# Score-table blanks on one DMA queue, and edge groups scored one place further up

## The chip, the cores and the metric

The kernel runs on one core of a Trainium2 chip. The metric is the device time of the whole program in microseconds, the median of several runs.

## The reference, cut to what matters

The program is two layers of a graph model on 625 nodes of width 256 with 20,000 edges. The first half of layer 0 holds two branches that share the engines. The edge branch gives each of the 20,000 edges four attention scores:

```python
e = xl[src] + xr[dst]                      # xl = xn @ W_l, xr = xn @ W_r
e = jnp.where(e >= 0, e, 0.2 * e)
score = jnp.einsum('ehd,hd->eh', e, att)   # then a softmax over the edges of each dst
```

The mix branch is dense: layer norm, `Wx`, a small linear attention over all nodes (`Wq`, `Wk`, `Wv`, `Wo`), a second layer norm, and a GELU MLP of width 1024. After these come the dense softmax of the edge scores, an expert layer, and the whole of layer 1; none of that is touched by the change.

## The kernel before, in words

The edges are cut into 32 groups of 5 x 125 edges. Groups 0 to 11 are "early": their scoring is written in between the pieces of the mix branch. Groups 12 to 31 are "late" and run in a loop of their own. All order is written by hand: each engine has one program in order and waits on semaphores.

An early group `g` takes these steps. `hot_rows(g)` on ACT turns the loaded destination indices into one-hot rows (10 activations, it needs `node_neg`). `early_rows(g, ...)` on PE multiplies them with `xr`, in three pieces of 20, 10 and 20 matmuls (line 481), into PSUM banks 5 to 7. POOL gathers the five columns of `xl[src]` from the DRAM table `xl_tab` (line 1778). DVE adds both (`add_rows`, line 909), applies the leaky ReLU and the weights and sums (`score_rows`, lines 887, 892, 895), and copies the indices of group `g + 2` (line 872). `score_early(g)` is both. POOL's `turn(g)` then scatters the scores of group `g - 2` to the DRAM tables `pair_scores` (line 1788) alternately with the gathers of group `g`, ten instructions in all:

```python
pool.wait_ge(sem("indices"), g + 1)
pool.wait_ge(sem("scored"), g - 1)
```

Both score tables (6.1 MB each) must first be filled with a large negative number. These are the blanks: ten DMAs of 1093.8 and 127.0 KB for each table, read from the SBUF tile `cnt`. POOL waits for both tables before its first scatter. Before the change SP sends the first table and ACT the second, after ACT has seen the `xl_tab` stores land.

`count_group(g, s)` on PE (line 459, 25 matmuls) counts edges per node pair from one-hots that DVE makes in `onehots(g, s)` (lines 944 and 945, ten instructions). PE does `count_group` 0 to 7 between the last early groups; a late group `g` on PE waits for the one-hots of group `g - 4`.

## Time and profile before

| what | value |
|---|---|
| median of 3 runs | 1266.75 us (1263.19 to 1271.56) |
| the profiled execution | 1262.88 us |
| its span, first to last instruction | 1261.1 us |
| PE busy | 961.6 us (76%) |
| DVE busy | 781.7 us (62%) |
| ACT busy | 468.5 us (37%) |
| POOL busy | 454.4 us (36%) |
| granted TensorE clock, mean | 0.876 of full speed |

The shares are averages over stages that differ. The change touches the stretch from 0 to about 250 us, so the windows and the chain of waits of that stretch tell more than the table. Times in the rows below are microseconds from the start of the span.

### The profile page before, as it was taken

To read this page: it belongs to the slowest core of one execution; us is meant where nothing else is said; L and a number is where in the kernel's file an instruction comes from. 1 tells how busy PE (TensorE), PEld (TensorE's weight loads), DVE (VectorE), ACT (ScalarE), POOL (GpSimd) and SP (SyncE) were. 2 spreads that over 40 slices of the span, in tenths; PEclk is the share of its full clock that TensorE was granted. 3 is DMA by queue.
4 is the path that set the end of the run, shared out by engine and by line. 5 is a ranking of instruction groups with operands and counts; after the bars stand their busy time and mean duration, and the time that the engine had idled before them with its cause. 6 is when DMAs were issued, how large, how long until landed. Compare 5 with 4: busy or idle time off the path is not lost.

```text
span 1261.1 us, 19695 instructions
## 1 busy us (share of the span) xinstructions
PE 961.6 (76%) x6816; PEld 836.3 (66%) x6816; DVE 781.7 (62%) x1821; ACT 468.5 (37%) x786; POOL 454.4 (36%) x371
## 2 busy tenths in 40 slices
PE   4387999699898988746328999908891982999992
PEld 2356887598797977546328899805781772788881
DVE  6368479777869889798663444234988757233312
ACT  2045756567766965255111111101540240111110
POOL 1448788877777778400002222140000000111103
PEclk9688999899999999957659999958895995899996
DMA  8932222222222222294036889840000003576662
GB/s 288 290 120 64 62 69 73 58 65 62 63 60 65 63 58 43 50 245 109 1 106 223 295 303 304 299 143 0 1 1 0 1 1 111 197 269 238 253 219 70
DMA packets 57996, 155.86 MB, mean 124 GB/s; under 512 B 23341, under 2 KB 33506, under 8 KB 49674
## 3 DMA queue, kind: packets, MB, share of 16 engines
q1 hardware_dynamic: 25500, 116.31, 28.0%
q0 software_dynamic: 25056, 24.10, 8.5%
q10 hardware_dynamic: 7378, 14.67, 3.5%
q8 instruction: 34, 0.56, 0.2%
q14 instruction: 28, 0.23, 0.1%
HBM read 133.82 MB, written 20.89 MB: 123 GB/s over the span
## 4 chain that ended last, share of the span: by engine, by line
PE 48%; DVE 22%; DMA 11%; issue 8%; POOL 6%; ACTq 2%; ACT 1%; another core or an unknown queue 0%; DVEq 0%; POOLq 0%; SPq 0%
PE bank L697 13%; PE bank L481 8%; PE bank L708 6%; DMA arena<-row_tab,ids 5%; DMA pair_scores<-sc_ring,idx_ring 4%; PE bank L645 4%; PE bank L459 4%; PE bank L443 3%; PE bank L433 3%; POOL arena L1778 2%; PE bank L634 2%; POOL pair_scores L1788 2%; POOL arena L1843 2%; ACTq L1586 2%; PE bank L762 1%
## 5 line engine op out<-in xcount | busy, mean ns | idle before, releaser
L1833 POOL DMA_INDIRECT arena<-row_tab,ids x42 | 58.7, 1398 | 573.9 <-DVE ids L1355 503.9
L1788 POOL DMA_INDIRECT pair_scores<-sc_ring,idx_ring x160 | 204.4, 1278 | 68.2 <-issue 48.8
L697 PE MATMUL bank<-arena 128*128 128x128 f32 (+1 forms) x1616 | 198.1, 280 | 0.0
L697 PEld LDWEIGHTS bank<-arena 128*128 128x128 f32 (+1 forms) x1616 | 186.3, 189 | 7.7 <-issue 3.6
L1778 POOL DMA_INDIRECT arena<-xl_tab,idx_ring x120 | 157.9, 1316 | 90.5 <-issue 33.2
L1367 DVE TENSOR_TENSOR arena<-bank,arena 128x512 f32<-128x512 f32 (+2 forms) x76 | 37.2, 509 | 151.9 <-ACT arena L1671 151.9
L708 PE MATMUL bank<-arena 128*128 128x256 f32 (+1 forms) x404 | 99.0, 388 | 0.0
L1558 ACT ACTIVATE late_ohT<-arena 125x875 fp32r<-125x875 f32 x100 | 90.7, 928 | 0.0
L1671 ACT ACTIVATE arena<-bank 128x512 f32<-128x512 f32 (+2 forms) x76 | 32.4, 450 | 148.1 <-PE bank L697 148.1
L481 PE MATMUL bank<-late_hi,late_ohT 125*125 125x256 f32 x500 | 85.9, 303 | 0.4 <-issue 0.3
L708 PEld LDWEIGHTS bank<-arena 128*128 128x128 f32 (+1 forms) x404 | 72.0, 190 | 16.6 <-issue 9.2
L459 PE MATMUL bank<-tde 125*128 125x314 bf16 x400 | 65.6, 318 | 19.9 <-DVE tde L945 19.0
L481 PE MATMUL bank<-late_lo,late_ohT 125*125 125x256 f32 x500 | 77.4, 285 | 0.1
L481 PEld LDWEIGHTS bank<-late_hi,late_ohT 125*125 125x125 f32 x500 | 70.4, 194 | 3.3 <-issue 0.5
L459 PE MATMUL bank<-tab 125*128 125x314 bf16 x400 | 61.3, 303 | 14.5 <-DVE tab L945 14.3
L1654 ACT ACTIVATE arena<-bank 128x256 f32<-128x256 f32 x42 | 16.1, 384 | 149.9 <-PE bank L684 135.4
L1626 ACT ACTIVATE arena<-arena,rneg 125x625 f32<-125x625 f32 (+4 forms) x60 | 44.8, 747 | 72.0 <-DVE rneg L1198 69.2
L481 PEld LDWEIGHTS bank<-late_lo,late_ohT 125*125 125x125 f32 x500 | 67.9, 190 | 0.5 <-issue 0.4
L645 PE MATMUL bank<-xlr,arena 125*125 125x96 f32 x400 | 57.9, 300 | 10.6 <-ACT arena L1634 10.5
L459 PEld LDWEIGHTS bank<-tde 125*128 125x128 bf16 x400 | 38.7, 103 | 38.0 <-DVE tde L945 21.0
L645 PEld LDWEIGHTS bank<-xlr,arena 125*125 125x125 f32 x400 | 55.1, 218 | 11.5 <-ACT arena L1634 11.2
L1345 DVE TENSOR_TENSOR arena<-iota_s,slot_rel 125x1280 f16<-125x1280 f16 x42 | 62.5, 1488 | 0.3
(307 smaller groups left out, 1923.6 us busy)
## 6 DMA issues: line engine op xcount, KB each, us to landing
arena<-in_exp SPq DMA_DIRECT2D x25, 1024.0 KB, 5.5
arena<-in_exp SPq DMA_DIRECT2D x17, 1364.0 KB
arena<-in_exp0o SPq DMA_DIRECT2D x25, 512.0 KB, 5.4
arena<-pair_scores SPq DMA_DIRECT2D x10, 1093.8 KB
arena<-in_exp1o SPq DMA_DIRECT2D x17, 640.0 KB
pair_scores<-cnt SPq DMA_DIRECT2D x5, 1093.8 KB
pair_scores<-cnt ACTq DMA_DIRECT2D x5, 1093.8 KB
slot_y<-arena ACTq DMA_DIRECT2D x42, 128.0 KB, 5.0
```

The lines of the kernel that those rows point to most:

```text
L433: mm = pe.matmul(bank[0:P, 0:width], f[:, k, t * P:(t + 1) * P], rhs(k), start=(k == 0), stop=(k == ks - 1))
L459: mm = pe.matmul(banks[m][:, 0:CW], oh_dst[s][:, j, m * P:m * P + 128], oh_src[s][:, j, :], start=start and j == 0, stop=True, skip_group_ ...
L481: mm = pe.matmul(banks[T + r][0:P, i * D:(i + 1) * D], hot[late, s][:, t, at * P:(at + 1) * P], part[:, t, :], start=(n == 0 and t == 0), ...
L645: mm = pe.matmul(banks[b][0:P, h * 128:h * 128 + VW], probT[:, i % 3, t * P:(t + 1) * P], v_rows(t, h), start=(t == 0), stop=(t == tiles_o ...
L697: mm = pe.matmul(banks[1 + 2 * q + buf][0:rows, i * SLOTS:(i + 1) * SLOTS], w_in(s, q, k, m, rows), xsT[:, s, k, :], start=(k == 0), stop= ...
L708: mm = pe.matmul(banks[5 + s][:, 0:D], hid[0:rows, s, m, :], w_out(s, m), start=(m == 0), stop=(m == len(flat) - 1))
L1345: v.tensor_tensor(sel[:, s, :, :], iota_s[:, :].unsqueeze(1).to_broadcast([P, 2 * T, SLOTS]), slot_rel[:, :].unsqueeze(2).to_broadcast([P, ...
L1558: ins = a.activation(hot[late, s][:, t - 1, :], apart[late, s][:, t - 1, :], ACT.Relu, scale=-1.0, bias=1.0)
L1626: a.activation(prob[:, i % 3, 0:w], masked[:, i % 3, 0:w], ACT.Exp, bias=rneg[:, i:i + 1], accum_out=rden[:, i:i + 1]).then_inc(sem(name + ...
L1778: p.indirect_dma_start(out=gat[:, b % 2, 0, j * D:(j + 1) * D], out_offset=None, in_=xl_tab, in_offset=bass.IndirectOffsetOnAxis(ap=idx_ri ...
L1788: p.indirect_dma_start(out=pair_scores[which], in_=sc_ring[:, b % 2, j, :], in_offset=None, out_offset=bass.IndirectOffsetOnAxis(ap=idx_ri ...
L1833: p.indirect_dma_start(out=xs[:, s, :], out_offset=None, in_=tab, in_offset=bass.IndirectOffsetOnAxis(ap=ids[:, s, :], axis=0))\
```

## The change

The blanks of the second table move from ACT's queue to SP's, behind the `xl_tab` stores and two loads of index rows, with three weight loads behind them (`vec0b`, `w0b`, `w2`). The twelve small loads of `mixw` and `mixk` move from SP's queue to the head of ACT's program, ahead of its first activation. The `xl_tab` store is cut into five per-tile stores. `node_neg` is made at the start, so that ACT can do `hot_rows(0)` and `hot_rows(1)` early. In the mix branch each early group is scored one place further up: group 0 before `mixhT` is copied out, group 1 before the `qv` copies, and so on. At the end of the early groups PE loses one place: `count_group(5)` now stands ahead of `early_rows(11)`.

```diff
@@ PE
-            pe.wait_ge(sem("w0_in"), 16)
             pe.wait_ge(sem("mixh"), 1)
             to_fm("mixhT", ta)
+            early_rows(1, 0, 1, 2)
+            pe.wait_ge(sem("w0_in"), 16)
...
-            early_rows(7, 0, 1, 2)
+            early_rows(8, 0, 1, 2)
             read_out(pe, "m2")
             count_group(0, 0)
             count_group(1, 1)
-            early_rows(8, 0, 1, 2)
+            early_rows(9, 0, 1, 2)
             count_group(2, 0)
             count_group(3, 1)
-            early_rows(9, 0, 1, 2)
+            early_rows(10, 0, 1, 2)
             count_group(4, 0)
-            early_rows(10, 0, 1, 2)
             count_group(5, 1)
             early_rows(11, 0, 1, 2)
             count_group(6, 0)
@@ DVE
+            dve.wait_ge(sem("iotas"), 5)
+            v.tensor_scalar(node_neg[:, :], node_f[:, :], -1.0, None, ALU.mult).then_inc(sem("node_neg"), 1)
             dve.wait_ge(sem("x_in"), 16 * len(PARTS))
...
             affine(ta, 0, "ln1_g", "ln1_b", sem("mixh"))
-            own.note(v.tensor_tensor(tb[:, :, :], xn[:, :, :], V(0, "bo"), ALU.add))
+            score_early(0)
             from_fm("mixhT", fb_)
...
-            score_early(0)
+            own.note(v.tensor_tensor(tb[:, :, :], xn[:, :, :], V(0, "bo"), ALU.add))
+            score_early(1)
...
-            score_early(9)
+            score_early(10)
             onehots(5, 1)
             take_counts(0, early, True)
-            score_early(10)
             onehots(6, 0)
+            score_early(11)
             onehots(7, 1)
-            score_early(11)
             onehots(8, 0)
@@ ACT
+            act.wait_ge(sem("mixw0"), 1)
+            for q in range(4):
+                rows = slice(32 * q, 32 * q + 32)
+                act.dma_start(mixw[rows, q, :], mixw_in[:, 0:KR + DH]).then_inc(sem("mixw_in"), 16)
+                for k in range(K2):
+                    at = (4 * k + q) * KR
+                    act.dma_start(mixk[rows, k, at:at + KR], mixw_in[:, KR + DH:]).then_inc(sem("mixw_in"), 16)
             from_fm("xnT0", fa)
             act.wait_ge(sem("node_neg"), 1)
             hot_rows(0, 0, 0)
-            act.wait_ge(sem("tables"), 16 * len(PARTS))
-            for m in range(T):
-                for rows in PARTS:
-                    act.dma_start(cells[1][m][rows], cnt[rows, :, :].rearrange("p m n -> p (m n)")[:, 0:H * NC])\
-                        .then_inc(sem("blank1"), 16)
...
+            hot_rows(1, 1, 0)
             from_fm("mixhT", fb_)
@@ SP
-            blank_first()
-            read_out(sp, "lr")
-            for rows in PARTS:
-                sp.dma_start(xl_tab.rearrange("(t p) d -> p t d", p=P)[rows], xlr[rows, :, 0:D])\
-                    .then_inc(sem("tables"), 16)
+            blank(0, range(T))
             sp.dma_start(vec[:, 0:V_FIRST], vec0_in[0:V_FIRST].partition_broadcast(128)).then_inc(sem("vec0_in"), 16)
+            for t in range(T):
+                read_out(sp, "lr", t)
+                for rows in PARTS:
+                    sp.dma_start(xl_tab[t * P:(t + 1) * P, :][rows], xlr[rows, t, 0:D]).then_inc(sem("tables"), 16)
...
             for g in range(2, 4):
                 edge_rows(g, g % 2, 0)
+            blank(1, range(T))
```

Three places of the program show it. The first is ACT's start, as a difference: line 1583 and 1586 are the small loads, `fa` receives the first transposed activations, which the product for `xl` and `xr` needs.

```order
 L1531 UNCONDITIONAL_BRANCH
+L1583 DMA mixw<-in_mixw 32x36
+L1586 DMA mixk<-in_mixw 32x4 x2
+L1583 DMA mixw<-in_mixw 32x36
+L1586 DMA mixk<-in_mixw 32x4 x2
+L1583 DMA mixw<-in_mixw 32x36
+L1586 DMA mixk<-in_mixw 32x4 x2
+L1583 DMA mixw<-in_mixw 32x36
+L1586 DMA mixk<-in_mixw 32x4 x2
 L1539 ACT_TABLE_LOAD
 L1539 ACTIVATE fa<-bank 128x375
```

Twelve DMA issues now stand ahead of the table load and the copy to `fa`.

The second is DVE behind the first layer norm of the mix branch. Before (`fb` receives `mixhT`, `fc` receives `Wx`'s output):

```order
L851 TENSOR_TENSOR tab<-tab,vec 125x1280 [waits dve_own]
L1050 TENSOR_TENSOR tab<-xn,vec 125x1280
L868 COPY fb<-bank 128x375 [waits full1]
L868 COPY fb<-bank 128x250 [waits full2]
L1055 TENSOR_SCALAR fc<-bank,fbias 128x375 [waits full0,fb_in]
L1055 TENSOR_SCALAR fc<-bank,fbias 128x250 [waits full1]
L909 TENSOR_TENSOR arena<-arena,bank 125x512 [waits z_made,gathered0]
```

Now:

```order
L851 TENSOR_TENSOR tab<-tab,vec 125x1280 [waits dve_own]
L909 TENSOR_TENSOR arena<-arena,bank 125x512 [waits z_made,gathered0]
L909 TENSOR_TENSOR arena<-arena,bank 125x512 [waits z_made]
L907 COPY bank<-vec 125x256 [waits z_made]
L909 TENSOR_TENSOR arena<-arena,bank 125x256
L887 SCALAR_TENSOR_TENSOR tc<-arena 125x1280 [waits edge_own,z_read]
L892 TENSOR_TENSOR tc<-tc,bank 125x1280 [waits edge_own]
L895 TENSOR_REDUCE sc_ring<-tc 125x20 [waits z_read]
L872 COPY idx_ring<-edge_ids 125x15
L868 COPY fb<-bank 128x375 [waits full1]
```

The scoring of group 0, with its wait for the gathers, moved ahead of the copy of `mixhT`.

The third is PE at the end of the early groups: `count_group(4)` (`tab`), `count_group(5)` (`tde`) and the one-hot products of an early group. Before:

```order
L459 MATMUL bank<-tab 128x314 [waits counts_read,onehot]
L459 MATMUL bank<-tab 128x314 x24
L481 MATMUL bank<-late_hi,early_ohT 125x256 [waits z_read,rows_hot]
L481 MATMUL bank<-late_hi,early_ohT 125x256 x4
L481 MATMUL bank<-late_lo,early_ohT 125x256 x5
```

Now:

```order
L459 MATMUL bank<-tab 128x314 [waits counts_read,onehot]
L459 MATMUL bank<-tab 128x314 x24
L459 MATMUL bank<-tde 128x314 [waits onehot]
L459 MATMUL bank<-tde 128x314 x24
L481 MATMUL bank<-late_hi,early_ohT 125x256 [waits z_read,rows_hot]
L481 MATMUL bank<-late_hi,early_ohT 125x256 x4
```

`count_group(5)` follows `count_group(4)` at once, and group 11's products stand behind it, where group 10's stood between them before.

## Rows read from the trace of the kernel before

**Rows 1.** Chain that ended last, 0 to 77 us: start, us, what

```profile
by line: ACTq L1586 26.8%; PE bank L433 14.1%; PE bank L443 9.3%; DMA x<-in_x 6.1%; ACT arena L1554 4.7%; issue 3.5%; ACT early_ohT L1558 3.1%; ACTq L1588 3.0%; ACTq L1592 3.0%; ACTq L1591 2.9%; DVE stats L838 2.3%; DVE arena L909 2.1%; DVE
...
15.42 10.85 PE bank L433 x20
...
61.89 7.13 PE bank L443 x16
```

**Rows 2.** Timeline, 0 to 60 us: start, us, engine, line, operation [idle before <-releaser]

```profile
0.81 1.28 ACT L1539 ACT_TABLE_LOAD   x1 [0.81 <-PEq L2048]
...
13.36 0.80 ACT L1539 ACTIVATE fa<-bank 128x375 f32<-128x375 f32 x2 [11.27 <-PE bank L424]
...
14.40 0.87 DVE L868 COPY fa<-bank 128x375 f32<-128x375 f32 x2
...
27.08 1.64 SPq L1885 DMA_DIRECT2D xl_tab<-xlr  x2
...
32.40 1.38 POOL L1778 DMA_INDIRECT arena<-xl_tab,idx_ring  x1 [24.92 <-DMA xl_tab<-xlr]
```

**Rows 3.** Timeline of the DMA issues on SP and ACT, and what ACT does next

```profile
5.34 15.37 SPq L1867 DMA_DIRECT2D pair_scores<-cnt  x10
...
7.12 13.59 SPq L1867 DMA_DIRECT2D pair_scores<-cnt  x7
...
47.83 6.12 SPq L1897 DMA_DIRECT2D mixk<-in_mixw  x2
...
33.70 20.31 ACTq L1586 DMA_DIRECT2D pair_scores<-cnt  x8
...
61.03 0.76 ACT L1539 ACTIVATE fb<-bank 128x375 f32<-128x375 f32 x2 [27.22 <-issue]
```

**Rows 4.** DMA queues, 33 to 63 us: packets, MB, share of 16 engines

```profile
q10 hardware_dynamic: 880, 6.84, 74.2%
q0 software_dynamic: 1141, 1.20, 11.6%
```

**Rows 5.** Timeline of POOL: first instruction of turns 2, 4 and 12

```profile
77.06 1.21 POOL L1778 DMA_INDIRECT arena<-xl_tab,idx_ring  x1 [28.42 <-DVE idx_ring L872]
...
109.95 1.23 POOL L1778 DMA_INDIRECT arena<-xl_tab,idx_ring  x1 [0.30 <-issue]
...
237.69 1.21 POOL L1788 DMA_INDIRECT pair_scores<-sc_ring,idx_ring  x1 [0.30 <-issue]
```

**Rows 6.** Timeline of DVE: groups 0, 1, 9, 10 and 11

```profile
69.43 1.28 DVE L909 TENSOR_TENSOR arena<-arena,bank 125x512 f32<-125x512 f32 x2
...
75.99 0.18 DVE L1062 COPY tde<-bank 125x32 f32<-125x32 f32 x1
...
93.60 0.16 DVE L872 COPY idx_ring<-edge_ids 125x15 int32<-125x15 int32 x1
...
207.06 1.61 DVE L909 TENSOR_TENSOR arena<-arena,bank 125x512 f32<-125x512 f32 x3
...
223.48 1.62 DVE L909 TENSOR_TENSOR arena<-arena,bank 125x512 f32<-125x512 f32 x3 [4.21 <-DMA arena<-xl_tab,idx_ring]
...
229.73 0.16 DVE L872 COPY idx_ring<-edge_ids 125x15 int32<-125x15 int32 x1
...
238.91 1.62 DVE L909 TENSOR_TENSOR arena<-arena,bank 125x512 f32<-125x512 f32 x3 [2.62 <-DMA arena<-xl_tab,idx_ring]
...
245.08 0.16 DVE L872 COPY idx_ring<-edge_ids 125x15 int32<-125x15 int32 x1
```

**Rows 7.** Timeline of PE, 205 to 265 us: the end of the early groups

```profile
216.60 5.18 PE L459 MATMUL bank<-tde 125*128 125x314 bf16 x25 [2.30 <-DVE tde L945]
224.32 1.40 PE L481 MATMUL bank<-late_hi,early_ohT 125*125 125x256 f32 x5 [2.53 <-DVE arena L909]
...
233.19 3.51 PE L459 MATMUL bank<-tab 125*128 125x314 bf16 x25 [1.19 <-DVE tab L945]
...
248.76 2.80 PE L459 MATMUL bank<-tab 125*128 125x314 bf16 x10 [6.36 <-DVE tab L945]
```

**Rows 8.** Window: stretch, its length, busy PE, PEld, DVE, ACT, POOL, then clock, DMA share, GB/s

```profile
180.00:200.00 20.00, 20.00 (x158) 16.54 (x157) 19.65 (x41) 7.50 (x13) 16.04 (x14) 1.00 0.28 62
```

More of the change, by code:

```diff
@@ L528, in _ @@
                 mm.then_inc(done, 1)
-            early_rows(1, 0)
+            early_rows(2, 0)
             pe.wait_ge(sem("ksoft"), 1)
@@ L541, in _ @@
                 mm.then_inc(done, 1)
-            early_rows(1, 1, 2)
+            early_rows(2, 1, 2)
             read_out(pe, "kN")
@@ L548, in _ @@
             mm.then_inc(done, 1)
-            early_rows(2, 0)
+            early_rows(3, 0)
             read_out(pe, "kv")
@@ L569, in _ @@
             hidden_mix(0, 1)
-            early_rows(4, 1, 2)
+            early_rows(5, 1, 2)
             hidden_mix(2, 3, 4)
-            early_rows(5, 0)
+            early_rows(6, 0)
             hidden_mix(5, 6, 7)
-            early_rows(5, 1, 2)
+            early_rows(6, 1, 2)
             read_out(pe, "m1")
@@ L1096, in _ @@
                 v.tensor_copy(fd[0:32, 1, off:off + w], bank[0:32, 0:w]).then_inc(freed, 1)
-            add_rows(1, 1, 2)
-            score_rows(1)
+            add_rows(2, 1, 2)
+            score_rows(2)
             bank, freed = got(dve, "kv")
@@ L1107, in _ @@
                 v.tensor_copy(fb_[:, 1, off:off + w], bank[:, 0:w]).then_inc(freed, 1)
-            add_rows(2, 1, 2)
-            score_rows(2)
+            add_rows(3, 1, 2)
+            score_rows(3)
             for t in range(T):
@@ L1129, in _ @@
             add_mix(0, 1)
-            add_rows(6, 0)
+            add_rows(7, 0)
             add_mix(2)
-            add_rows(6, 1, 2)
-            score_rows(6)
+            add_rows(7, 1, 2)
+            score_rows(7)
             add_mix(3, 4)
@@ L1138, in _ @@
             onehots(1, 1)
-            score_early(7)
+            score_early(8)
             onehots(2, 0)
             onehots(3, 1)
-            score_early(8)
+            score_early(9)
             onehots(4, 0)
@@ L1595, in _ @@
             biased("xm", fc, FB_BX)
-            hot_rows(1, 1, 0)
+            hot_rows(2, 0, 0)
             act.wait_ge(sem("kmax"), 1)
@@ L1601, in _ @@
             a.activation(te[:, :, 0:32], te[:, :, 0:32], ACT.Exp).then_inc(sem("qexp"), 1)
-            hot_rows(2, 0, 0)
+            hot_rows(3, 1, 0)
             for c, (off, w, _) in enumerate(CHUNKS):
@@ L1605, in _ @@
                 a.activation(fb_[:, 0, off:off + w], bank[:, 0:w], ACT.Copy).then_inc(freed, 1)
-            hot_rows(3, 1, 0)
             hot_rows(4, 0, 0)
+            hot_rows(5, 1, 0)
             from_fm("h2T", fb_)
             biased("m1", mlp, FB_B1, ACT.Gelu, range(0, 2))
-            hot_rows(5, 1, 0)
+            hot_rows(6, 0, 0)
             biased("m1", mlp, FB_B1, ACT.Gelu, range(2, 8))
-            for g in range(6, 10):
+            for g in range(7, 11):
                 hot_rows(g, g % 2, 0)
             read_counts(0)
-            hot_rows(10, 0, 0)
             split_counts(0)
@@ L1804, in turn @@
                         gather(g, b, FETCHED[FETCH_AFTER.index(j)])
-            pool.wait_ge(sem("tables"), 16 * len(PARTS))
+            pool.wait_ge(sem("tables"), T * 16 * len(PARTS))
             for g in range(2):
@@ L1862, in _, with blank @@
                 sp.dma_start(dsti[rows], dst_in[rows]).then_inc(sem("edges_in"), 16)
-            def blank_first():
-                for m in range(T):
+            def blank(w, tiles):
+                for m in tiles:
                     for rows in PARTS:
-                        sp.dma_start(cells[0][m][rows], cnt[rows, :, :].rearrange("p m n -> p (m n)")[:, 0:H * NC])\
-                            .then_inc(sem("blank0"), 16)
+                        sp.dma_start(cells[w][m][rows], cnt[rows, :, :].rearrange("p m n -> p (m n)")[:, 0:H * NC])\
+                            .then_inc(sem(f"blank{w}"), 16)
             def edge_rows(g, s, late):
@@ L1890, in _ @@
             sp.dma_start(wres[:, :, n_lr:n_w1], w0_in[:, :, n_lr:n_w1]).then_inc(sem("w0_in"), 16)
-            sp.wait_ge(sem("mixw0"), 1)
-            for q in range(4):
-                rows = slice(32 * q, 32 * q + 32)
-                sp.dma_start(mixw[rows, q, :], mixw_in[:, 0:KR + DH]).then_inc(sem("mixw_in"), 16)
-                for k in range(K2):
-                    at = (4 * k + q) * KR
-                    sp.dma_start(mixk[rows, k, at:at + KR], mixw_in[:, KR + DH:]).then_inc(sem("mixw_in"), 16)
             for g in range(2, 4):
                 edge_rows(g, g % 2, 0)
+            blank(1, range(T))
+            sp.dma_start(vec[:, V_FIRST:V_SIZE0], vec0_in[V_FIRST:].partition_broadcast(128))\
+                .then_inc(sem("vec0b_in"), 16)
+            sp.dma_start(wres[:, :, n_w1:W_SIZES[0]], w0_in[:, :, n_w1:]).then_inc(sem("w0b_in"), 16)
+            sp.dma_start(w2, w2_in).then_inc(sem("w2_in"), 16)
             for g in range(4, LATE):
```

25 lines of the change are left out of this document (9 added, 16 removed).

## The prediction

> **What bounds the kernel now.** I read the stretch that the change touches, 0 to 250 us, first in the chain of waits, then in the timelines of the engines that it names. From 0 to 77 us the chain is led by ACT's queue: issuing the blanks of the second table (line 1586) alone is 26.8% of that stretch, against 14.1% for the product that makes xl and xr [rows 1]. The timeline shows how. ACT issues eight of its ten blank DMAs in 20.31 us, then three weight loads, and only at 61.03 copies mixhT, after 27.22 us in which it computed nothing [rows 3]. PE runs Wx's product from 61.89 [rows 1], DVE scores group 0 from 69.43 [rows 6], and POOL, which waits 28.42 us for that, starts turn 2 at 77.06 [rows 5]. Meanwhile the DMA engines are nearly full: from 33 to 63 us ACT's queue takes 74.2% of them and the gathers 11.6% [rows 4].
>
> From 77 us on POOL hardly waits: turns 2 to 11 take it to 237.69 [rows 5], 16.1 us each. But it is not the bound alone. From 180 to 200 us PE is busy for all 20.00 us and DVE for 19.65 [rows 8]; the MLP of the mix branch fills PE there. So a start of POOL that is X us earlier is worth X only as far as PE and DVE can follow. At the end, DVE waits 4.21 and 2.62 us for gathers of groups 10 and 11 [rows 6], so all three meet within a few microseconds. After 248.76, where PE starts the first counts of a late group [rows 7], PE and DVE pace the late groups, and I take that loop, and everything after it, as unchanged. The question is when this 248.76 comes.
>
> **The start: twelve small loads on ACT.** They begin when mixw is cleared, about 4.5 us. SP's blanks begin at once too. Three of SP's ten blanks go between 5.34 and 7.12, 0.6 us each, then the queue fills: seven take 13.59 us, 1.94 us each [rows 3]. A small load is slowed with them, though it lies on the other queue: SP's last two mixk loads took 6.12 us for 0.5 KB each while ACT issued blanks [rows 3], 3.06 us each, as long as the blanks beside them. So of the twelve about six are out by 7.12, and the other six go one for one with blanks, 11.6 us: ACT is free at 18.7. Its table load of 1.28 us, at 0.81 before, now follows, and the copy to fa starts at 20.0 in place of 13.36 [rows 2]. It takes 0.80 us, and DVE's copy ended at 15.27 [rows 2], so the product starts 5.4 us late. The bounds: nothing, if all twelve go at the rate of the first blanks (0.6 us each, done by 11.7, under 13.36 with the table load to spare or nearly so); 7.5 us, if they last as long as SP's ten blanks (20.7). I take 5.
>
> The Trainium skill, DMA: Bandwidth & Descriptors, section Queues, rings and completion order, says that each DMA engine takes its queue rows in turn, a packet at a time, so that small loads on ACT's row should slip in between SP's blanks. By that the delay would be nothing, and the sum at the end about 3 us better. The 6.12 us row speaks against it: the issuing side waits, whatever the engines do.
>
> **The tables and gathers.** Before, the stores to xl_tab began at 27.08 and POOL gathered from 32.40 [rows 2], 5.3 us later. Per-tile stores leave only the last tile behind the last copy, which saves about 2 us; with the 5 us delay the gathers start at 35.5, 3 us late. Before, the ten gathers of groups 0 and 1 (1.28 MB) had moved 1.20 MB by 63 us, beside 6.84 MB on ACT's queue [rows 4], so 0.08 MB landed later still, up to 20 us after the last gather was issued. With the same sharing group 0 is in at about 53 and group 1 at about 72.
>
> **Blanks of table 1.** On SP they follow the stores, w0 and the index rows of groups 2 and 3; these wait for hot_rows(0) and (1), which ACT now does by about 34. I put the first blank at 35, where ACT's was 32.6. The same bytes in the same company put the last at about 65. The rest of SP's queue (weights, rows of group 4) is needed much later, from about 96 us on. POOL's turn 2 then starts at 65, not 77.06: 12 us early. Bounds: 59.5, when group 0 is scored (17 us early), and 72, if the blanks are served last.
>
> **The mix branch.** DVE now waits for group 0's gathers at 53, needs 6.6 us for the scoring (69.43 to the qv copies at 75.99 before [rows 6]), and copies mixhT at 60. Wx's product starts at 60.5, against 61.89; so freeing ACT gives the mix branch only 1 us. It ends at 66 to 67. Group 1's scoring stands next and waits for its gathers: 72 to 78.6. The qv copies come 2.6 us later than before. I take the mix branch 3 us late from there, range -2 to +8. What has been gained is that group 1 is done at that point. Before, it was done at 93.7 [rows 6], and turn 4 began at 109.95 [rows 5]. Now group 2 is done at about 96.5, 3 us behind that 93.7; turn 4 can start at 97, 13 us early. From there POOL runs 13 us ahead at its own 15 to 16 us a turn, if the following groups keep the one place.
>
> **The end of the early groups.** Here the place is lost again. Before, DVE made the one-hots of group 5 ahead of scoring group 10, now behind it, and PE counts group 5 ahead of group 11's products. With POOL 13.3 us ahead, the gathers of group 10 land at 210.2 (223.48 before [rows 6]), and DVE, 3 us late in the mix branch, is free at about the same time (it began group 9 at 207.06 [rows 6]). One after another: group 10 scored, 6.4 us (223.48 to 229.89 [rows 6]): 216.7. One-hots of group 5, 3.2 us (group 8's, 245.24 to 248.76 [rows 6, 7], less a handover): 219.9. PE, which did groups 9 and 10 by about 212, has waited some 8 us, and its count takes 5.18 us as after the idle of 2.30 [rows 7], not 3.51: 225.1. Fifty products of group 11, 7.0 us between the 6.2 at full clock and the 7.7 of [rows 7] (224.32 to 232.0): 232.1. DVE's last piece and scoring, 5 us: 237. One-hots of group 7, 3.2 us: 240.3. Its count, 3.5 to 5.2 us, and the first piece of group 12, 2.2 us (233.19 + 2 x 3.51 = 240.2 to 248.76 - 6.36 = 242.4): 246 to 247.7. Before, PE got there at 242.4 and waited to 248.76 [rows 7] for one-hots of group 8, which now come at 243.5. So the late groups start 1 to 3 us early; I take 3, since a clock that stays up is worth that. Of POOL's 13 us, 10 turn into new waits of PE for one-hots.
>
> **The sum.** 1262.88 of the profiled execution less 3 is 1259.9. The median of the runs lies 3.87 above that execution, so I forecast 1263.8.
>
> **Rivals.** First: POOL's lead reaches the end. It needs DVE to have its one-hots done while it waits for gathers, as it did before in 4.21 and 2.62 us [rows 6], and a mix branch no later than before. Then the late groups start 10 to 13 us early: 1254 to 1257. Against it stands the order on DVE, in which one-hots 5 and 7 now follow the scoring.
>
> Second, slower: the start delay. If ACT's small loads last to 20.7 and the gathers of group 1, in the same full engines, land at 78 rather than 72, the mix branch is 8 or more us late. PE has no idle time from 140 to 214 in which to catch up (as in 180 to 200 [rows 8]), so DVE scores group 10 at 215 or later, the chain above shifts by 5, and the late groups start 2 to 5 us late: 1268 to 1272. It decides where the mix branch is more than 6 us late. For it speaks that it needs only one queue effect already seen; against it that PE's products of group 1 are already done then.
>
> Third, nothing moves: the DMA engines are nearly full in either order [rows 4], and only the name of the waiting engine changes. POOL starts at 72 or later, and the end comes within 1 us: 1266 to 1267. The Trainium skill, same page, section Issuing engines are not separate DMA queues, has this as a rule: DMAs of all issuers run on the same sixteen engines, and a second issuer saves only issuing time, usually small. The trace agrees on the bytes and not on "small" (20.31 us for eight issues [rows 3]).
>
> **How the numbers follow.** Forecast 0.45, first rival 0.2, second 0.2, third 0.15. A measurement of this kernel can tell about 1% (12.7 us) from no change. Faster by more than that needs all of POOL's lead: 0.15, within 1% 0.77, slower 0.08. The range reaches from the whole lead, 1253, to 1273, where the slower rival has its bound on top of the spread of the runs.
>
> **What would show it.** In the new trace: the fa copy on ACT at 18 to 20; ACT's copy of mixhT not preceded by 27 us of issue; turn 2 at 65, turn 4 at 97; the qv copies at 78 to 79; PE idle ahead of count_group(5) and (7) on one-hots; the first count of a late group at 246. The prediction is wrong if the small loads on ACT go at full rate, or if group 1's gathers land well before 70: then the mix branch itself comes forward, and with it all that follows.

## The result and the profile after

The changed kernel takes 1271.72 us, the median of 20 runs (1268.02 to 1277.69); the kernel before, on the same chip, 1263.51 (20 runs, 1255.37 to 1274.34). The ratio is 1.0075, with a 95% interval of 1.006 to 1.009: slower, clear of noise, where I had forecast 1263.8. That forecast stood 3 us below the 1266.75 that three runs of the kernel before had given; its median over 20 runs is 3.2 us lower, so the forecast was 3 us faster and the change came out 8.2 us slower. The profiled execution took 1271.35 us with a span of 1269.6.

The chain of waits of the kernel after, 0 to 77 us (start, us, what), answers to [rows 1]:

```profile
by line: DMA arena<-xl_tab,idx_ring 30.0%; ACTq L1586 18.4%; PE bank L433 14.8%; POOL arena L1775 7.5%; PE bank L481 7.1%; ACTq L1583 6.6%; issue 5.5%; DVE cnt L1018 3.5%; DMA xl_tab<-xlr 2.0%; ACT fa L1539 1.0%; DVE xlr L1041 0.9%; DVE are
...
13.04 4.35 ACTq L1586
...
24.01 0.12 ACT L1539
...
26.27 11.42 PE bank L433 x20
```

ACT's queue still leads into the product that makes xl and xr, but now with its small loads (lines 1583 and 1586), one of which takes 4.35 us to issue. Behind the product comes a name that was not in the chain before: the gathers of xl_tab, 30.0% of the stretch.

Timelines of the kernel after, 0 to 85 us (start, us, engine, line, operation, idle time before and its releaser), answer to [rows 2, 3, 5, 6]:

```profile
4.47 0.41 ACTq L1583 DMA_DIRECT2D mixw<-in_mixw  x1
...
5.34 17.43 SPq L1864 DMA_DIRECT2D pair_scores<-cnt  x10
...
10.68 6.71 ACTq L1586 DMA_DIRECT2D mixk<-in_mixw  x2
...
24.01 1.28 ACT L1539 ACT_TABLE_LOAD   x1 [24.01 <-issue]
...
40.67 2.12 POOL L1775 DMA_INDIRECT arena<-xl_tab,idx_ring  x1 [33.21 <-DMA xl_tab<-xlr]
...
41.41 16.60 SPq L1864 DMA_DIRECT2D pair_scores<-cnt  x10
...
52.08 0.76 ACT L1539 ACTIVATE fb<-bank 128x375 f32<-128x375 f32 x2 [12.83 <-PE bank L424]
...
70.75 1.28 DVE L909 TENSOR_TENSOR arena<-arena,bank 125x512 f32<-125x512 f32 x2 [19.31 <-DMA arena<-xl_tab,idx_ring]
...
78.39 1.21 POOL L1775 DMA_INDIRECT arena<-xl_tab,idx_ring  x1 [21.32 <-DVE idx_ring L872]
```

Three things are to be seen. The small loads keep ACT until 24.01. The first gather comes at 40.67 instead of 32.40 [rows 2], just ahead of the blanks of table 1 at 41.41, and DVE waits 19.31 us for group 0 to be in. And although ACT has its half of mixhT copied at 52.08 (it was 61.03 [rows 3]), DVE scores group 0 from 70.75 and copies its own half only after that. POOL's turn 2, at 78.39, is no earlier than the 77.06 of [rows 5].

At the end of the early groups the timeline of PE, 215 to 270 us, answers to [rows 7]; SP's load of the finished score tables, which ends the loop over the late groups, stands below it:

```profile
222.99 3.51 PE L459 MATMUL bank<-tab 125*128 125x314 bf16 x25
234.70 5.94 PE L459 MATMUL bank<-tde 125*128 125x314 bf16 x25 [8.20 <-DVE tde L945]
...
255.27 5.89 PE L459 MATMUL bank<-tde 125*128 125x314 bf16 x25 [5.37 <-DVE tde L945]
...
263.38 1.51 PE L459 MATMUL bank<-tab 125*128 125x314 bf16 x10
...
538.93 40.60 SPq L1906 DMA_DIRECT2D arena<-pair_scores  x20
```

PE waits 8.20 us for the one-hots of group 5 and 5.37 for those of group 7. The first counts of a late group come at 263.38, 14.6 us later than 248.76 [rows 7]. The same load of the tables stands in the kernel before as:

```profile
529.91 40.62 SPq L1912 DMA_DIRECT2D arena<-pair_scores  x20
```

So of the 14.6 us 9.0 are left at the end of the loop, and 8.5 in the spans (1269.6 against 1261.1).

### The profile page after: what moved, and what is told of

The parts are those of the page before. It is cut to its first block, busy times and chain, and to the rows that moved or that the text cites. A ratio compares the mean times of both kernels' runs of the same rounds, so it can differ in the third digit from the quotient of the medians.

```text
span 1269.6 us, 19702 instructions
## 1 busy us (share of the span) xinstructions
PE 965.3 (76%) x6816; PEld 837.4 (66%) x6816; DVE 779.3 (61%) x1821; ACT 468.0 (37%) x786; POOL 453.0 (36%) x371
## 4 chain that ended last, share of the span: by engine, by line
PE 54%; DVE 24%; DMA 10%; issue 6%; POOL 3%; ACTq 2%; ACT 1%; DVEq 0%; POOLq 0%; SPq 0%
PE bank L697 12%; PE bank L481 12%; DMA arena<-row_tab,ids 6%; PE bank L708 6%; PE bank L459 5%; PE bank L645 4%; PE bank L433 3%; PE bank L443 3%; DMA arena<-xl_tab,idx_ring 2%; PE bank L634 2%; POOL arena L1840 2%; PE bank L762 1%; PE bank L503 1%; DVE tc L887 1%; PE bank L495 1%
## 5 line engine op out<-in xcount | busy, mean ns | idle before, releaser
L459 PE MATMUL bank<-tde 125*128 125x314 bf16 x400 | 69.8, 331 | 29.9 <-DVE tde L945 29.8
L481 PE MATMUL bank<-late_hi,early_ohT 125*125 125x256 f32 x300 | 51.6, 306 | 22.0 <-DVE arena L909 18.1
```

What stands on the lines that cost most here:

```text
L459: mm = pe.matmul(banks[m][:, 0:CW], oh_dst[s][:, j, m * P:m * P + 128], oh_src[s][:, j, :], start=start and j == 0, stop=True, skip_group_ ...
L481: mm = pe.matmul(banks[T + r][0:P, i * D:(i + 1) * D], hot[late, s][:, t, at * P:(at + 1) * P], part[:, t, :], start=(n == 0 and t == 0), ...
```

## The experiments

Each time is a median, each ratio one to the kernel before, run on the same chip in the same series; the numbers in brackets are its 95% interval. The series ran on different chips, where the kernel before had medians from 1258.26 to 1261.65, so kernels of different series are compared by their ratios. Besides the time, two marks of the profile are read: the first counts of a late group (248.76 before, 263.38 after), and the load of the tables (529.91 and 538.93). Each mark is of one execution, and that one is not always near the median: it took 5.0 us less in e3, 4.0 less in e8, 3.4 less in e15, 5.7 less in e13 and 7.7 more in e10. A few microseconds between the marks of two kernels prove nothing by themselves.

### The small loads

**e1_small_back.** In the changed kernel, the twelve small loads go back to SP, behind w0:

```diff
@@ ACT
-            act.wait_ge(sem("mixw0"), 1)
-            for q in range(4):
-                ... (the twelve loads)
             from_fm("xnT0", fa)
@@ SP
             sp.dma_start(wres[:, :, n_lr:n_w1], w0_in[:, :, n_lr:n_w1]).then_inc(sem("w0_in"), 16)
+            sp.wait_ge(sem("mixw0"), 1)
+            ... (the twelve loads)
```

> The changed kernel with one part undone: the twelve small loads of mixw and mixk go back to SP, behind the load of w0; all else stays. Start theory (the small loads at the head of ACT, held up one for one by SP's blanks, make the product for xl and xr 10.9 us late, and that lateness is the loss): the product starts at 15.4, gathers at 31 to 33, and the time falls by 8 to 11 us against the changed kernel, to that of the kernel before or a little under it. Order theory (the loss is DVE's wait for the gathers of group 0, now ahead of the copy of mixhT): the start comes forward as said, but DVE still waits until the gathers land at 60 or later, Wx's product starts at 69 or later, and the time stays 3 to 8 us above the kernel before.

Measured: 1265.99 us, ratio 1.0034 [1.0011, 1.0058]. The product starts at 15.24, the first gather at 36.20, group 0 is scored from 58.90. First late count 255.70, tables 531.96: 7.7 and 7.0 us earlier than after. PE's waits at the tail stay (11.34 us before count_group(5), 5.37 before count_group(7)). The time lies where the order theory had it, 4.3 us above the kernel before, though the theory's cause did not hold: e6 below takes DVE's wait for group 0 out of the way of Wx's product and gains nothing that can be told. Half of the loss is the place of the small loads; the other half is somewhere else.

**e2_small_only.** In the kernel before, only those twelve loads move to the head of ACT.

> The kernel before with one part of the change alone: the twelve small loads at the head of ACT's program. Start theory: the product for xl and xr starts at 26 in place of 15.4, everything behind it shifts by 9 to 11 us, and most of it reaches the end: plus 8 to 11 us against the kernel before. Order theory: the late start costs less than 4 us at the end, because PE's wait from 42 to 62 takes it up.

Measured: 1270.47 us, ratio 1.0072 [1.0045, 1.0099]. The product starts at 26.75, the first gather at 42.32; first late count 259.49, tables 540.53. This is the start theory: the edit alone costs 10.6 us at the tables, where the whole change costs 9.0.

**e7_blanks_wait.** In the changed kernel, SP waits for the small loads before it issues a blank:

```diff
@@ SP
             sp.wait_ge(sem("blank"), 1)
+            sp.wait_ge(sem("mixw_in"), 12 * 16)
             blank(0, range(T))
```

> The changed kernel, but SP waits for the twelve small loads (on ACT, at the head) before it issues the first blank. Theory A, the small loads are slow because SP's blanks are issued beside them: all twelve are out within 5 to 7 us (0.45 us each), ACT's table load starts by 12, the lr product at 15 to 16 instead of 26.27, and the time is that of e1_small_back or up to 3 us above it, since blanks and stores come some 6 us later: 1265 to 1269. Theory B, twelve loads on ACT's queue take some 20 us whatever runs beside them: the table load stays at 23 to 25, and as the blanks come after it, the time is 1272 or more.

Measured: 1274.16 us, ratio 1.0101 [1.0073, 1.0129]. Its timeline of ACT's, SP's, POOL's and DVE's queues:

```profile
4.91 0.91 ACTq L1586 DMA_DIRECT2D mixk<-in_mixw  x2
...
10.13 1.28 ACT L1539 ACT_TABLE_LOAD   x1 [10.13 <-issue]
...
11.43 17.43 SPq L1864 DMA_DIRECT2D pair_scores<-cnt  x10
...
31.22 6.24 SPq L1884 DMA_DIRECT2D xl_tab<-xlr  x10
...
40.64 1.86 POOL L1775 DMA_INDIRECT arena<-xl_tab,idx_ring  x1 [33.16 <-DMA xl_tab<-xlr]
...
71.31 1.28 DVE L909 TENSOR_TENSOR arena<-arena,bank 125x512 f32<-125x512 f32 x2 [30.05 <-DMA arena<-xl_tab,idx_ring]
```

Theory A holds for the loads: without blanks beside them twelve take 5.7 us, 0.47 each, not 19.5. Its time was wrong, and this is the more useful half. The product starts at 15.50, as before, and still nothing is gained, since the stores of xl_tab now stand on SP's queue behind blanks that go until 28.86 and a load of vec; and as ten stores per tile they take 6.24 us to issue, where two took 1.64 [rows 2]. The first gather comes at 40.64, where it was at 40.67. The gathers start as late when the stores' queue is full as when the product is late. How long the small loads take to land agrees with how long they take to issue: the median of the eight `mixk` loads is 8.3 us from issue to landing in the kernel after, and 3.0 here.

**e12_small_behind_fa.** e5_tail_back (below) with the loads on ACT behind its copy to fa.

> e5_tail_back with the twelve small loads on ACT behind its copy to fa and ahead of its first hot rows, instead of on SP behind w0. Theory A, only the place at ACT's head costs: the lr product starts at 15.3 as in e5, the loads go at 2 us each only until SP's blanks are out (about 23), then 0.45 us each, ACT is free at 21 to 25 and its hot rows are ready before xr is; SP starts the blanks of table 1 some 5 us earlier than 39.86, turn 2 comes at 67 to 70: 1252 to 1256. Theory B, the lockstep is met again, by the stores as well, and ACT's hot rows come 5 us or more late, so that group 0's products start at 36 or later: 1257 to 1261.

Measured: 1257.44 us, ratio 0.9982 [0.9959, 1.0006]. Theory B: the loads take from 13.71 to 30.96, slowed again by what SP issues beside them. Nothing on the path to the product stands behind them, and it starts at 15.35, but ACT's hot rows do, so the products of group 0 start at 37.92, where e5 has them at 30.20. SP did not gain: its index rows waited for ACT's hot rows, and the blanks began at 44.78, later than the 39.53 of e5. Only group 0 came earlier, at 49.46, and that gave no time.

### The gathers of group 0

**e11_blanks1_held.** e5_tail_back with the blanks of table 1 behind the landing of group 0's gathers:

```diff
@@ SP
+            sp.wait_ge(sem("gathered0"), G * 16)
             blank(1, range(T))
```

> e5_tail_back, but SP waits for all five gathers of group 0 before it issues the blanks of table 1. Theory A, group 0's gathers are late (DVE starts on them at 56.67, 23 us after the first is issued) because the blanks' bytes run beside them: without those they are in at 44 to 48, Wx's product starts at 52 to 57 instead of 64.83; the blanks end some 5 us later and POOL's turn 2 comes at 76 to 80 instead of 72.56; time 1254 to 1259. Theory B, the gathers take 20 us or more by themselves, or beside what is left of table 0's blanks: group 0 stays at 54 or later, the blanks end at 78 or later, and the time is 1258 to 1264.

Measured: 1254.04 us, ratio 0.996 [0.9943, 0.9977]; group 0 is in at 46.51, 11.1 us after the first gather. Theory A, and the kT product comes at 71.68 where e5 has it at 80.72; but the time is not to be told from e5's (0.9949), since DVE then waits 10.19 us for the gathers of group 2, which turn 2 issues only at 73.37, after the blanks of table 1. The other runs have the same events with other gaps. Worked out from the start of the first gather, of the first blank of table 1 and of DVE's first sum of group 0, where DVE waited for gathers:

| kernel | first gather | first blank of table 1 | group 0 in | gather to in |
|---|---|---|---|---|
| after | 40.67 | 41.41 | 70.75 | 30.1 |
| e7_blanks_wait | 40.64 | 39.61 | 71.31 | 30.7 |
| e9_tail_only | 39.60 | 40.29 | 69.30 | 29.7 |
| e4_old_order | 37.95 | 38.74 | 68.50 | 30.6 |
| e8_old_order_small_first | 40.22 | 39.31 | 67.69 | 27.5 |
| e1_small_back | 36.20 | 39.86 | 58.90 | 22.7 |
| e5_tail_back | 33.94 | 39.53 | 56.67 | 22.7 |
| e3_blanks_only | 32.47 | 36.83 | 53.85 | 21.4 |
| e12_small_behind_fa | 37.17 | 44.78 | 49.46 | 12.3 |
| e11_blanks1_held | 35.39 | 46.50 | 46.51 | 11.1 |

In e6, e10 and e15, with gaps of 4.7 to 5.7 us, it is 22.8 to 23.3, in e13, held as in e11, 10.9. The five gathers are issued in 8.2 us (the kernel after, 40.67 to 48.86). Blanks that start with them make the landing 19 us later than blanks that start when they are in. Between e5 and the kernel after, a start of the gathers that slips from 34 to 41 us costs 14 us at group 0 (56.67 to 70.75), twice the slip. The gap is not the whole of it: 3.7 us (e1) and 5.6 (e5) both give 22.7. The page's view of the DMA queues, 33 to 63 us, after first and e11 below (queue: packets, MB, share of 16 engines):

```profile
q1 hardware_dynamic: 1904, 6.58, 73.5%
q0 software_dynamic: 518, 0.53, 5.1%
```

```profile
q1 hardware_dynamic: 2012, 5.82, 61.2%
q0 software_dynamic: 1275, 1.29, 16.5%
```

The kernel before is not in the table, since DVE did not wait for group 0 there, but its bytes can be read. This is the same view for the 20 us from the first gather on, of the kernel before (32.40 to 52.40) and the kernel after (40.67 to 60.67):

```profile
q10 hardware_dynamic: 521, 4.34, 72.6%
q1 hardware_dynamic: 830, 0.64, 11.8%
q0 software_dynamic: 784, 0.80, 11.7%
```

```profile
q1 hardware_dynamic: 1082, 5.45, 91.3%
q0 software_dynamic: 431, 0.45, 6.5%
```

The blanks start 0.2 us after the first gather in the one (32.63) and 0.7 in the other, yet the gathers have moved 0.80 MB and 0.45 MB. e2, whose blanks go from ACT's queue as before and start 1.0 us after the first gather, has moved 0.73. So what SP issues beside the gathers leaves them less than what ACT issued. Whether that is by the queue or by what else is issued on it no run separates.

**e13_turn2_one_table** (e11 with the scores of groups 0 and 1 all in table 0) and **e14_held_group0_behind** (e11 with group 0 scored behind DVE's copies of mixhT) asked what comes next once group 0 is early.

> e11_blanks1_held (1254.04 us), but the scores of groups 0 and 1 all go to table 0 (SINGLE 2 instead of 0), so that turns 2 and 3 wait for the blanks of table 0 alone. Theory A, the blanks of table 1 set when group 2 is fetched, and group 2's gathers set the mix branch: turn 2 starts when group 0 is scored, at 56 to 58 instead of 73.37, DVE's wait of 10.19 us ahead of group 2's rows falls below 3, the mix branch and the tail come 5 us or more earlier, 1246 to 1250. Theory B, scatters to one table wait for each other, and the blanks' bytes then slow group 2's gathers: the wait stays above 6 and the time is 1252 to 1258.

> e10_tail_group0_behind (1251.09 us) and e11_blanks1_held (1254.04) in one: Wx's product ahead of group 0's scoring, and the blanks of table 1 behind group 0's gathers. Theory A, neither is on the path any more, because group 2's gathers are waited for: DVE's wait ahead of group 2's rows is 8 us or more, the time 1251 to 1255. Theory B, they add: 1246 to 1250.

Measured: 1260.38, ratio 1.0023 [0.9996, 1.0051], and 1254.55, 0.996 [0.994, 0.998]. Turn 2 of e13 does start at 54.20, but its second scatter waits 12.09 us for the first to land, the next two 5.34 and 3.69, and DVE still waits 10.89 us for the gathers of group 2, and 11.12 for those of group 3, which are issued between the scatters. The wait is the program's: `scatter` waits for the semaphore of the table that it writes. Theory B holds in its mechanism; the time is above its 1252 to 1258. In e14 DVE waits 12.46 us for group 2; theory A. What group 0 gains is waited for again at group 2.

### The place of the groups and the tail

**e6_group0_behind.** e1_small_back with group 0 scored behind DVE's copies of mixhT and of Wx's product.

> e1_small_back with the scoring of group 0 behind DVE's copies of mixhT and of Wx's product (PE does Wx's product ahead of group 1's products); groups 1 to 11 keep the changed kernel's places. Theory A, DVE waiting for group 0's gathers ahead of the mixhT copy is what makes the mix branch late: Wx's product starts at 43 to 46 instead of 67.99, the kT product comes 5 us or more ahead of 81.00, first late count about 250, time 1259 to 1262. Theory B, the branch is held by group 1's scoring, which stands ahead of the qv copies in both and waits for its own gathers: Wx's product is early, but kT stays at 79 to 82, and the time within 2 us of 1266.

Measured: 1264.62 us, ratio 1.0019 [0.9995, 1.0044]. Theory B: Wx's product starts at 42.00, 26 us earlier than in e1, and the kT product at 80.75 against 81.00. Group 1's scoring stands ahead of the qv copies in both. **e10_tail_group0_behind** is the same on e5: 1251.09 us, 0.994 [0.9919, 0.9962], with six runs. The time is the one that theory B gives below, but the interval overlaps e5's, and in the profiled execution, which was the slowest of the six, the kT product comes at 83.47, no earlier than e5's 80.72. It stays open.

> e5_tail_back (1255.83 us) with group 0 scored behind DVE's copies of mixhT and Wx's product, as in e6_group0_behind. Theory A, Wx's product was never on the path, since group 1's scoring stands ahead of the qv copies in either: kT stays at 80 to 81 and the time within 2 us of 1255.8. Theory B, the earlier product is worth what e6 showed at most beside e1 (1.4 us, 1265.99 to 1264.62) and more where the tail no longer hides it: 1251 to 1254.

**e5_tail_back.** e1_small_back, with the tail's order on DVE put back:

```diff
@@ DVE
             v.tensor_tensor(xl_lo, xl, xl_hi.bitcast(F32), ALU.subtract).then_inc(sem("xl_parts"), 1)
-            score_early(10)
             onehots(5, 1)
             take_counts(0, early, True)
+            score_early(10)
             onehots(6, 0)
-            score_early(11)
             onehots(7, 1)
+            score_early(11)
             onehots(8, 0)
```

> The changed kernel with its twelve small loads back on SP behind w0 (as in e1_small_back, 1265.99 us), and in the tail the one-hots of group 5 and the first take_counts again ahead of scoring group 10, the one-hots of group 7 ahead of group 11. Theory A, the tail's order costs what PE waits there (11.34 us ahead of count_group(5), 5.37 ahead of count_group(7) in e1_small_back): the first wait falls to 2 to 4 us and the second vanishes, the first late count comes 5 us or more earlier than 255.70, time 1258 to 1261. Theory B, the waits are only where DVE, late from the mix branch, is waited for in either order: PE then waits as long for rows or z of groups 10 and 11, the first late count stays within 2 us of 255.70, time 1264 to 1267.

Measured: 1255.83 us, ratio 0.9949 [0.9922, 0.9975]. PE's two waits of e1 first, then PE's timeline of e5, and SP's load of the tables:

```profile
226.89 6.03 PE L459 MATMUL bank<-tde 125*128 125x314 bf16 x25 [11.34 <-DVE tde L945]
...
247.55 5.94 PE L459 MATMUL bank<-tde 125*128 125x314 bf16 x25 [5.37 <-DVE tde L945]
```

```profile
212.50 3.51 PE L459 MATMUL bank<-tab 125*128 125x314 bf16 x25
218.16 3.51 PE L459 MATMUL bank<-tde 125*128 125x314 bf16 x25 [2.15 <-DVE tde L945]
...
230.63 5.18 PE L459 MATMUL bank<-tab 125*128 125x314 bf16 x25 [2.90 <-DVE tab L945]
235.65 3.50 PE L459 MATMUL bank<-tde 125*128 125x314 bf16 x25
...
244.02 2.06 PE L459 MATMUL bank<-tab 125*128 125x314 bf16 x10 [2.50 <-DVE tab L945]
...
523.22 40.63 SPq L1906 DMA_DIRECT2D arena<-pair_scores  x20
```

Theory A, and more than it expected. Two moves of one-hots, 3 us of work each (the first take_counts goes with the first of them), bring the first late count 11.7 us forward and the tables 8.7. The wait before count_group(5) falls from 11.34 to 2.15 us, that before count_group(7) is gone; and both counts take 3.5 us, not the 6.03 and 5.94 that they took in e1 after the idle time.

**e9_tail_only.** The same edit in the changed kernel, with the small loads left at ACT's head.

> The changed kernel whole (small loads at the head of ACT, 1271.72 us), with only the tail's order put back: one-hots of group 5 and the first take_counts ahead of scoring group 10, those of group 7 ahead of group 11. Theory A, tail order and late start are separate costs: the tail gives back what it gave beside e1_small_back (10 us: 1265.99 to 1255.83), so 1260 to 1263, with the first late count near 253 to 255. Theory B, they cover each other (a branch that is 18 us late makes PE and DVE meet in either order): it gives 5 us or less, 1266 to 1270.

Measured: 1260.29 us, ratio 1.0014 [0.9993, 1.0036]; first late count 252.46, tables 529.74: 10.9 and 9.2 us earlier than after. Theory A: the tail's order gives 0.6% beside late loads and 0.85% beside e1, the loads' place 0.4% with the tail's new order and 0.65% without it. As far as the intervals can tell the two causes add, and neither hides the other.

**e4_old_order.** The changed kernel's DMAs with the whole scoring order of before; **e15_old_order_small_back**, e5's DMAs with it; **e3_blanks_only**, the kernel before with nothing but the blanks of table 1 and the three weight loads on SP, behind the small loads; **e8_old_order_small_first**, e4 with the small loads on SP ahead of the first blank.

> The changed kernel with its scoring order undone on PE, DVE and ACT: groups stand where they stood before; all moves of DMAs, the early node_neg and the early one-hot rows of group 1 stay. Order theory: Wx's product starts at about 54 in place of 79.5, though the start is still 10.9 us late, and the time falls 8 to 14 us below the changed kernel. Start theory: the 10.9 us late start still rules, and the time falls by no more than 3 us.

> e5_tail_back (1255.83 us) with the scoring order of before on PE, DVE and ACT; the same DMAs in the same places. Theory A, one place up is worth nothing by itself once the tail's order is that of before: 1254 to 1257. Theory B, it gives what POOL's lead promised: the old order is 4 us or more slower, 1260 or above. A third outcome, 1251 or below, would mean that the place itself costs.

> The kernel before with one part alone: the blanks of the second table and the three weight loads go from ACT's queue to SP's, behind the small loads. The order of the groups stays. Both theories: ACT copies mixhT at about 43 in place of 61, Wx's product starts at 44. Order theory: the mix branch then runs some 8 to 15 us ahead, since nothing waits for gathers ahead of Wx, and the time falls 5 to 12 us below the kernel before. Start theory: the start is as before, so the time is that of the kernel before or at most 4 us less, because the DMA engines are full to 70 us and POOL starts when it did.

> The changed kernel's DMAs with the scoring order of before (as e4_old_order, 1261.83 us), and the small loads on SP ahead of the first blank. Theory A, what kept e4_old_order behind e3_blanks_only (1257.0) is the 9 us late lr product: the product starts at 15.3, gathers at 29 to 32, first late count at 240 to 243, time 1254 to 1257. Theory B, the ten per-tile stores and the earlier hot rows cost as much as they give, or the first blanks, 5.5 us later, reach into the time of the stores: 1258 to 1262.

| kernel | us | ratio | first gather | first late count | tables |
|---|---|---|---|---|---|
| e4 | 1261.83 | 1.0002 [0.9975, 1.0028] | 37.95 | 250.95 | 528.28 |
| e15 | 1254.44 | 0.9972 [0.9953, 0.9992] | 35.13 | 244.07 | 519.04 |
| e3 | 1257.0 | 0.9973 [0.9946, 1.0001] | 32.47 | 242.90 | 520.99 |
| e8 | 1265.25 | 1.0038 [1.0014, 1.0061] | 40.22 | 250.41 | 528.40 |

e15 beside e5 differs in the groups' place alone: the first late count is the same (244.07 and 244.02), and the ratios' intervals overlap. That is theory A of e15. e4 beside e9 is the same pair with the small loads at ACT's head, and says the same: 1.0002 and 1.0014, first late count 250.95 and 252.46. So the 9.9 us by which e4 lies below the changed kernel are the tail's and not the place's. Its order theory forecast them, together with an early Wx product (51.88), but e9 has the product at 77.75 and lies as low. The place is worth nothing that these runs can tell, once the tail's order is right. e3 moves only the blanks and three weight loads to SP and has the same ratio as e15, so the blanks on SP are probably the part that gains, and no gain of the stores per tile or the early hot rows shows; but e3's own interval ends at 1.0001. e8 came out above both its theories, by the mechanism of e7: with the product on time at 15.49, the stores wait behind blanks and the gathers start at 40.22.

The best kernel by its interval is e10 or e5, 0.5 to 0.6% faster than before; e11, e14 and e15 lie within reach of them.

## Why the prediction was wrong

The step that failed is the landing of the gathers and, resting on it, the lead of POOL. The prediction had group 0 in at 53, turn 2 at 65 and POOL 13 us ahead from there, and it paid 10 us of new waits at the tail out of that lead. Measured were 70.75, 78.39 and no lead; and the tail's order then cost what had been taken as paid.

The account, in us at the first late count and, in brackets, at the load of the tables; each term is the difference between two runs:

| term | from | us |
|---|---|---|
| small loads at ACT's head | after less e1 | +7.7 (+7.0) |
| one-hots behind the scoring at the tail | e1 less e5 | +11.7 (+8.7) |
| all the rest: blanks on SP, stores per tile, early hot rows, the place | e5 less before | -4.7 (-6.7) |
| sum | after less before | +14.6 (+9.0) |

The ratios of the times give the same three terms, as +0.41, +0.85 and -0.51 per cent, sum +0.75. The measured time lies inside the range of 1253 to 1273 and within the 1% of the likeliest class, but it moved the other way than forecast, by a mechanism that had been given a chance of 0.2.

Point by point:

- **The start, wrong in size and beyond its bound.** I took 5 us, at most 7.5. The product came 10.85 us late. I let six loads out at full rate and the other six go one for one with blanks at 1.94 us; four had full rate (0.4 us each), and the rest took from 1.03 to 4.35 each while SP's ten blanks took 17.43 us instead of 15.37. The sign of the mechanism was right, and e7 shows that it is the blanks beside them. The Trainium skill, DMA: Bandwidth & Descriptors, section Queues, rings and completion order, says that a DMA engine takes its rows in turn, a packet at a time. That small loads would therefore slip in was my conclusion, and it did not give the time here: 19.5 us for twelve loads beside blanks, 5.7 alone. The same page's section Issuing engines are not separate DMA queues says that a second issuer saves only issuing time, usually small beside the transfer. e2, which moves nothing but who issues twelve loads, costs 0.7%: not by what the transfers take, but because ACT's copy to `fa` stands behind the issues. What no run tells is what the issuing side waits for.
- **The gathers, the step that failed most.** "With the same sharing group 0 is in at about 53": it was 70.75. The start of 35.5 was 40.67, and with a product on time it is still 33.94 to 36.20 in the runs with stores per tile (e1, e5, e15), 32.47 with two stores (e3): the 2 us that I had let the stores per tile save are lost in issuing them. And the time to land was 30.1 us, not 17.5. No row gave the 17.5: [rows 4] held both groups up to 63 us. For the kernel before it fits all the same, as half of the 1.28 MB had moved some 18 us after the first gather (0.51 MB after 16 us, 0.80 after 20). What failed is "the same sharing": with the blanks on SP the gathers got 0.45 MB in 20 us. And the table above shows that the landing also hangs on how far ahead of the blanks the gathers start.
- **Blank 1 and POOL's lead.** I had turn 2 at 65 and POOL 13 us ahead from there. Turn 2 came at 78.39, after DVE had group 0 scored, and turn 4 at 111.40 against my 97 and the 109.95 of [rows 5]. There was no lead to lose. Nor is the late start all of it: with the loads back on SP, turn 2 waits for the blanks of table 1 until 70.64 (e1) and 72.56 (e5), about my bound of 72, and turn 4 comes at 103.44 and 104.44. That is a lead of 5.5 to 6.5 us, half of the 13.
- **The mix branch, wrong by its input.** "3 us late, range -2 to +8": the kT product came at 92.51 in place of 76.56, 16 us late. Of that e1 leaves 4.4 (81.00), so 11.5 are the start's. And putting group 0 ahead of mixhT, which I had costed as a wait to 60, held Wx's product to 79.50; e6 shows that this alone was not the bound, since group 1's scoring stands next.
- **The tail, right as a mechanism, wrong in the books.** I forecast a wait of some 8 us before count_group(5) and one before count_group(7): 8.20 and 5.37. The chain from the scoring of group 10 to the first late count took what I had worked out, 32.0 us (from 231.4, where the last sum of group 10 ends, 229.94 and 1.49, to 263.38) against 29.3 (216.7 to 246). I had the chain start at 210.2, where group 10 is scored; it started at 225.18, 1.7 us later than the 223.48 of [rows 6]. These 15.0 us are most of the 17.4 between my 246 and the 263.38. I had paid for the tail from POOL's lead, which had to be there first. Without it the 10 us that I had "turned into new waits" are a loss; e5 and e9 measure them as 8.7 and 9.2 at the tables.
- **The loop after it.** Taken as unchanged; it gave 5.6 us back (275.6 us from the first late count to the tables, 281.2 before). The profile's groups show one part: from 280 to 500 us PE waits 12.6 us for one-hots before its counts; in the kernel before it waited 15.6. The rest was not looked into.
- **The rivals.** The second came true in its sign and its cause, the start delay. I had put it at 0.2. That its 1268 to 1272 holds the 1271.72 is partly luck: it had the late groups start 2 to 5 us late and they start 14.6 late, of which the loop gives 5.6 back, and its times stand on a median of 1266.75 that was 3.2 us high. It also named the gathers of group 1, and DVE does not wait for those (group 1 is added from 85.70, without a wait) but for group 0. The first rival named what e5 then showed: with the one-hots done while DVE would wait, the change gains.

## What to carry to other kernels

Before a small DMA is put at the head of a compute engine's program, look at what the other queues issue beside it: here an issue took up to 4.35 us where it takes 0.47 alone, and it holds the engine. Gathers that somebody waits for land earlier when a bulk stream starts behind them (11.1 us against 30.1 here), though e11 gained no time by it, as the next wait took it up. Read the landing of the first gather from a kernel in which somebody waits, or from the bytes moved. In an engine that works in order, work that is ready belongs ahead of work that waits for a transfer; a wait that is paid from a lead should be costed with the lead at nothing as well.

## What was not expected of the hardware

- Twelve loads of 0.5 to 4.5 KB take ACT 5.7 us to issue alone and 19.5 us while SP issues blanks of 127 KB and 1094 KB (e7 and after), single ones up to 4.35 us. The eight of 0.5 KB land 3.0 and 8.3 us after their issue, by the median.
- Five gathers of 125 rows land 11.1 us after the first is issued where no blanks run beside them from that queue, and 27.5 to 30.7 us after it where SP starts its ten blanks within 1.1 us of it (after, e4, e7, e8, e9). With blanks on ACT's queue as close behind, the gathers move 0.73 to 0.80 MB in 20 us, not 0.45 (e2, before, after).
- How long a scatter of 125 score rows takes to land can be read where the program makes the next one wait for it, in e13: the waits are 12.09, 5.34 and 3.69 us between the first four, beside the blanks, and from 89.17 us on between 0.30 and 1.20. No run has scatters that alternate between the tables beside the blanks.
- A count of 25 matmuls takes 3.51 us where PE was busy before it. After 2.08 to 2.98 us of idle time it takes 3.51 in some places (count_group(5) in e5) and 4.91 to 5.18 in others (before, e9), and after 5.37 to 11.34 us 5.89 to 6.46 (after, e1, e6, e7). The windows of the kernel after show the granted clock (length, busy PE, PEld, DVE, ACT, POOL, clock, DMA share, GB/s). The last three are count_group(4), which follows busy time, and the two that follow waits, 5 and 7. With a mean of 0.58 over their length, most of each of the two runs at the lower of the two levels, 1.2 GHz.

```profile
200.00:220.00 20.00, 20.00 (x160) 17.03 (x159) 19.65 (x40) 7.47 (x14) 16.04 (x14) 1.00 0.29 65
220.00:240.00 20.00, 11.80 (x74) 8.44 (x73) 19.79 (x36) 17.37 (x22) 16.33 (x13) 0.74 0.32 79
240.00:260.00 20.00, 14.63 (x99) 11.34 (x98) 13.96 (x31) 0.00 (x0) 15.53 (x12) 0.83 0.20 40
...
222.99:226.50 3.51, 3.51 (x27) 2.37 (x25) 3.48 (x5) 3.51 (x6) 2.87 (x3) 1.00 0.23 48
234.70:240.64 5.94, 5.94 (x27) 3.65 (x28) 5.94 (x12) 2.70 (x4) 5.02 (x4) 0.58 0.39 94
255.27:261.16 5.89, 5.89 (x27) 3.62 (x28) 3.13 (x10) 0.00 (x0) 4.67 (x5) 0.58 0.16 26
```
